# Combine weights by way of DRAM, fewer and larger loads, bias copies over three engines, layer norms applied on VectorE

## The reference

```
x = x + Xattn0(LN(x), ctx, mask)     16 heads of 8, relative bias, key mask
x = x + FFN(LN(x))                   low-rank: gelu(x U1 V1 + b1) U2 V2 + b2
x = x + Xattn1(LN(x), ctx)           16 heads of 8, no bias and no mask
x = x + MoE(LN(x))                   16 experts, hidden 64, top 8, and one shared expert
```

## Time and profile before

| | |
|---|---|
| median of three runs | 346.16 us (345.96 to 347.55) |
| the profiled execution's own time | 346.3 us |
| its span, first to last instruction | 343.8 us |
| PE busy | 182.1 us, 53% |
| DVE busy | 112.8 us, 33% |
| ACT busy | 106.7 us, 31% |
| POOL busy | 95.0 us, 28% |
| mean granted TensorE clock | 0.77 |

### The profile page before, as it was taken

One profiled execution on the slowest core, in us unless ns is written; L12 is line 12 of the kernel. 1 busy time (PEld: TensorE's weight loads), 2 busy tenths in 40 slices (PEclk: granted clock), 3 DMA queues, 4 the chain that ended last, 5 costly groups with the idle time before them and its releaser, 6 DMA issues.

```text
span 343.8 us, 4955 instructions
## 1 busy us (share of the span) xinstructions
PE 182.1 (53%) x1875; PEld 124.8 (36%) x1875; DVE 112.8 (33%) x273; ACT 106.7 (31%) x189; POOL 95.0 (28%) x179
## 2 busy tenths in 40 slices
PE   2059189849995989700089600099699200460006
PEld 1045034436652556600078500077478100450006
DVE  5224755318558457600004300037655200010000
ACT  1016556726551758600036300034543100010000
POOL 5508531014652143000295000342153000500014
PEclk9999589969995699965559965569899755585557
DMA  5796632223022112877501877511003877277760
GB/s 153 238 183 133 127 79 56 50 61 86 20 51 57 26 45 55 29 42 35 19 0 8 33 36 33 60 38 47 11 2 11 33 35 34 11 27 36 39 36 15
DMA packets 33078, 17.96 MB, mean 52 GB/s; under 512 B 12032, under 2 KB 32352, under 8 KB 33056
## 3 DMA queue, kind: packets, MB, share of 16 engines
q1 hardware_dynamic: 33056, 17.66, 46.6%
HBM read 5.04 MB, written 0.55 MB: 16 GB/s over the span
## 4 chain that ended last, share of the span: by engine, by line
PE 30%; SPq 24%; issue 22%; DMA 11%; POOL 5%; DVE 5%; ACT 2%; POOLq 0%
SPq L270 14%; PE two_s L1151 5%; DMA cbS<-combT 5%; SPq L248 5%; PE two_s L1143 4%; PE one_m L1285 4%; SPq L206 4%; PE two_s L1258 3%; PE one_m L1197 2%; DMA stack_Q<-nmT 2%; POOL hid_h L469 2%; PE one_m L1229 2%; PE one_m L1093 2%; POOL xn L424 2%; PE one_m L1119 2%
## 5 line engine op out<-in xcount | busy, mean ns | idle before, releaser
L469 POOL TENSOR_TENSOR hid_h<-hid_h,cbS 128x512 f32<-128x512 f32 x16 | 20.0, 1268 | 133.3 <-DMA cbS<-combT 133.3
L882 DVE TENSOR_REDUCE mx<-two_s 128x8 f32<-128x1024 f32 x32 | 38.1, 1220 | 50.3 <-PE two_s L1151 49.9
L1285 PE MATMUL one_m<-wd,hid_h 128*128 128x128 f32 x128 | 21.5, 332 | 57.0 <-POOL hid_h L469 57.0
L1285 PEld LDWEIGHTS one_m<-wd,hid_h 128*128 128x128 f32 x128 | 20.0, 242 | 58.5 <-POOL hid_h L469 57.3
L602 ACT ACTIVATE pt_p<-two_s 128x1024 f32<-128x1024 f32 x32 | 32.0, 1024 | 24.7 <-PE two_s L1151 24.5
L1093 PE MATMUL one_m<-ident,xn 128*128 128x128 f32 x32 | 7.4, 318 | 59.2 <-POOL xn L424 58.7
L550 ACT ACTIVATE xnT<-one_m 128x256 f32<-128x256 f32 x16 | 6.1, 383 | 70.7 <-PE one_m L1093 70.7
L1093 PEld LDWEIGHTS one_m<-ident,xn 128*128 128x128 f32 x32 | 3.8, 154 | 62.2 <-POOL xn L424 60.2
L424 POOL TENSOR_SCALAR xn<-xr,mv,rstd 128x128 f32<-128x128 f32 x32 | 25.9, 817 | 1.7
L939 DVE TENSOR_TENSOR hid_h<-hid_h,two_s 128x512 f32<-128x512 f32 x16 | 10.9, 683 | 39.2 <-ACT hid_h L640 33.9
L1197 PE MATMUL one_m<-pt_p,va 128*32 128x128 f32 x512 | 21.5, 296 | 0.2 <-ACT pt_p L602 0.2
(11 more groups left out here) (116 smaller groups left out, 325.2 us busy)
## 6 DMA issues: line engine op xcount, KB each, us to landing
cbS<-combT SPq DMA_DIRECT2D x64, 64.0 KB, 7.9
stack_K<-ksp SPq DMA_DIRECT2D x48, 64.0 KB, 2.1
stack_Q<-qsp SPq DMA_DIRECT2D x48, 64.0 KB, 2.1
cbS<-rel_bias_scratch SPq DMA_DIRECT2D x3, 224.0 KB, 4.1
wg<-in_wg SPq DMA_DIRECT2D x1, 544.0 KB, 4.0
wu<-in_wu SPq DMA_DIRECT2D x1, 544.0 KB, 4.8
xr<-in_x SPq DMA_DIRECT2D x4, 128.0 KB, 3.4
cx<-in_ctx SPq DMA_DIRECT2D x4, 128.0 KB, 2.8
```

The source lines that it names most:

```text
L469: pool.tensor_tensor(h[:].rearrange("p (c t) -> p c t", c=2), h[:].rearrange("p (c t) -> p c t", c=2), cbS[:, p % 2, 2 * u:2 * u + 2], ALU ...
L882: free(dve.tensor_reduce(mx[:, l, p % 2, b, c].rearrange("p a j -> p (a j)"), src[:].rearrange("p a (j k) -> p (a j) k", j=4), AX.X, ALU.m ...
L1285: ins = pe.matmul(dst[:, b * D:(b + 1) * D], h[:, at_col:at_col + SEQ], wd[:, 2 * u + k], start=False, stop=(n == UNITS), skip_group_check ...
```

## The change

Seven things change.

1. `combT` of a pair is stored to DRAM by one DMA (`store_weights`, 16 KB), and after that has landed two DMAs of 512 KB, each reading every second expert's row 64 times over, fill `cbS` (`spread_weights`).
2. `normalize` is parted: POOL keeps the power (`power`), DVE applies the norm, for all four norms. The forms for POOL and ACT that the text of the kernel also has (`normalize` there, `shift_of`) are called by nothing.
3. The loads are merged: identity, constants and the Q and K biases are one DMA (`first`), which ACT issues together with `wqk`; wv, wo, bv and b1 are one (`second`); the low-rank factors and the gate (`small`), wg and wu (`wgu`), wd and swd (`wdown`), pairs 1 to 3 of x and of ctx are one each. SP issues 10 loads. Context and x of pair 0 come early, `small` last.
4. The mask comes repeated over heads from DRAM, in uint8, and two DMAs that POOL issues write it as bf16 into `bias_s` and `bias_t`; the copy on DVE and the eight DMAs on SP are gone.
5. Of the eight window copies DVE makes four (two of each kind), ACT two and POOL two (one of each kind); PE waits for all three engines before the first use of each kind.
6. Four of the eight stacks are cleared on POOL instead of DVE.
7. The lists of all five engines and of the PSUM and SBUF slots are written in a new order. In POOL's, the powers of the norms of pairs 2 and 3 stand ahead of the `weigh` calls, but for `power(2, 3)`; in SP's, the stacking of Q for pair 3 stands ahead of the second spread; in PE's, the `down` calls of pair 1 stand beside the gates of pair 2.

The diff, cut to its core (the slot table and most of the reordered lists are left out):

```diff
+    comb_d = nc.dram_tensor("combine_scratch", (2, EXPERTS, TOK), F32, kind="Internal").ap()
...
+            def store_weights(p):
+                freed(sp, f"ct{p}")
+                sp.dma_start(comb_d[p % 2], combT[:, p % 2]).then_inc(sem("comb_stored"), 16)
+
             def spread_weights(p):
-                freed(sp, f"ct{p}")
+                sp.wait_ge(sem("comb_stored"), 16 * (p + 1))
                 if p >= 2:
                     sp.wait_ge(sem("weighted"), UNITS * (p - 1))
-                for e in range(EXPERTS):
-                    r = 64 * (e % 2)
-                    src = combT[e:e + 1, p % 2].unsqueeze(1).broadcast_to([1, 64, TOK])
-                    sp.dma_start(cbS[r:r + 64, p % 2, e // 2], src).then_inc(sem(f"spread{p % 2}_in"), 16)
+                for k in range(2):
+                    src = bass.AP(tensor=comb_d.tensor, offset=(p % 2) * EXPERTS * TOK + k * TOK,
+                                  ap=[[0, 64], [2 * TOK, ECH], [1, TOK]])
+                    sp.dma_start(cbS[64 * k:64 * k + 64, p % 2], src).then_inc(sem(f"spread{p % 2}_in"), 16)
...
-            load(table, table_d, "rel")
-            load(onehot, onehot_d, "rel")
-            load(wqk[:], wqk_d, "wqk")
-            load(bqk[:], bqk_d, "wqk")
+            load(rel_in, rel_in_d, "rel")
             load(rowb[:], rows_d.partition_broadcast(128), "rows")
-            load_x(0)
-            load(wv[:], wv_d, "wv")
-            load(wo[:], wo_d, "wo")
-            load(bv[:], bv_d, "wo")
-            load_x(3)
-            load_x(2)
-            load_x(1)
-            load(mask8[96:128, 0], masks_d.rearrange("(g r) k -> r g k", g=4), "mask")
-            load(mask8[96:128, 1], maskt_d.rearrange("(g r) k -> r g k", g=4), "mask")
-            load_ctx(1)
-            load_ctx(3)
-            load(u1t, u1t_d, "ffw")
-            load(v1, v1_d, "ffw")
-            load(u2t, u2t_d, "ffw")
-            load(v2, v2_d, "ffw")
-            load(b1[:], b1_d, "ffw")
-            load_ctx(2)
-            load(gate, gate_d, "gate")
-            load(wg[:], wg_d, "moe")
-            load(wu[:], wu_d, "moe")
-            load(wd[:], wd_d, "moe")
-            load(swd[HID:128], swd_d, "moe")
-            load(ident[:], ident_d, "ident")
-            load(consts[:].bitcast(U16), consts_d, "consts")
-            load_ctx(0)
+            load_x(1, 4)
             fixed_rows(0, 0)
+            load_ctx(0, 1)
+            load_x(0, 1)
+            load(second[:], second_d, "second")
+            fixed_rows(0, 1)
+            load(wgu[:], wgu_d, "wgu")
+            store_windows()
             fixed_rows(1, 0)
-            spread_masks()
-            store_windows()
-            stack("K", 0, 1, 0)
+            load_ctx(1, 4)
+            load(wdown[:], wdown_d, "wdown")
+            load(small, small_d, "small")
             stack("K", 0, 0, 0)
             load_windows()
...
+            store_weights(0)
             spread_weights(0)
-            spread_weights(1)
             stack("Q", 0, 1, 2)
             stack("Q", 1, 1, 2)
             stack("Q", 2, 1, 2)
+            store_weights(1)
             stack("Q", 0, 1, 3)
+            stack("Q", 2, 1, 3)
+            max_rows(1, 2, 0)
             stack("Q", 1, 1, 3)
-            stack("Q", 2, 1, 3)
+            spread_weights(1)
             store(0)
-            max_rows(1, 2, 0)
-            store(1)
             max_rows(1, 2, 1)
             max_rows(1, 3, 0)
             max_rows(1, 3, 1)
+            store_weights(2)
             spread_weights(2)
+            store(1)
+            store_weights(3)
             spread_weights(3)
             store(2)
             store(3)
...
+            def load_masks():
+                for t in range(2):
+                    pool.dma_start(bias["ST"[t]][96:128], masks_d[t].rearrange("r (g h k) -> r g h k", g=4, h=HEADS))\
+                        .then_inc(sem("masks_in"), 16)
...
-            def normalize(n, p):
+            def power(n, p):
                 if n == 0 and p == 0:
                     pool.wait_ge(sem("half"), 1)
                 pool.wait_ge(sem(f"variance{n}"), p + 1)
                 pool.tensor_tensor(rstd[:, p], ve[:, p], half[:], ALU.pow).then_inc(sem(f"rstd{n}"), 1)
...
-            constants()
+            negative_half()
+            clear_stack("K01")
+            clear_stack("Q01")
             clear_values(0, 0)
             clear_values(0, 1)
             scale_queries()
-            normalize(0, 0)
+            clear_max()
+            power(0, 0)
+            load_masks()
+            power(0, 1)
+            power(0, 2)
+            gate_power()
             residual(0, 0)
             residual(0, 1)
             residual(0, 2)
             residual(0, 3)
-            normalize(0, 1)
-            normalize(0, 2)
-            normalize(0, 3)
-            gate_power()
-            window_t(1)
-            window_t(3)
-            split_max(0, 0, 0)
+            window("T", 3)
+            power(0, 3)
+            window("S", 3)
+            clear_stack("K11")
+            clear_stack("Q11")
             clear_values(1, 0)
             clear_values(1, 1)
...
-            normalize(3, 0)
+            power(3, 0)
             router_norm(0)
             residual(1, 2)
-            normalize(1, 2)
+            power(1, 2)
+            residual(1, 3)
+            power(1, 3)
+            residual(2, 2)
+            power(2, 2)
+            power(3, 1)
             weigh(0, 0)
-            normalize(3, 1)
+            weigh(0, 1)
             router_norm(1)
-            residual(1, 3)
-            weigh(0, 1)
-            normalize(1, 3)
+            residual(2, 3)
             weigh(0, 2)
-            residual(2, 2)
-            normalize(2, 2)
+            power(2, 3)
             weigh(0, 3)
-            residual(2, 3)
-            weigh(1, 0)
-            normalize(2, 3)
-            weigh(1, 1)
-            weigh(1, 2)
             split_max(1, 2, 0)
-            weigh(1, 3)
             split_max(1, 2, 1)
             split_max(1, 3, 0)
+            weigh(1, 0)
+            weigh(1, 1)
             split_max(1, 3, 1)
-            normalize(3, 2)
+            weigh(1, 2)
+            power(3, 2)
+            weigh(1, 3)
             router_norm(2)
-            normalize(3, 3)
+            power(3, 3)
             router_norm(3)
             weigh(2, 0)
...
+            act.dma_start(first[:], first_d).then_inc(sem("first_in"), 16)
+            act.dma_start(wqk[:], wqk_d).then_inc(sem("wqk_in"), 16)
...
+            def normalize(n, p):
+                dve.wait_ge(sem(f"rstd{n}"), p + 1)
+                for b in range(2):
+                    ins = dve.tensor_scalar(xn[:, p, b], xr[:, p, b], mv[:, p, b, 0:1], rstd[:, p, b:b + 1],
+                                            ALU.subtract, ALU.mult)
+                ins.then_inc(sem(f"norm{n}"), 1)
...
+            clear_stack("K00")
             clear_stack("Q00")
-            clear_stack("K00")
+            clear_stack("K10")
             clear_stack("Q10")
-            clear_stack("K10")
             variance(0, 0)
-            mask_bf16()
-            value_bias()
-            clear_stack("Q01")
-            second_ffn()
             variance(0, 1)
             variance(0, 2)
+            variance(0, 3)
             gate_clamp()
-            variance(0, 3)
-            clear_stack("K01")
-            clear_stack("Q11")
-            clear_stack("K11")
-            window_s(0)
-            window_s(1)
-            window_s(2)
-            window_s(3)
+            value_bias()
+            normalize(0, 0)
+            normalize(0, 1)
+            normalize(0, 2)
             gate_scale()
+            second_ffn()
+            window("S", 0)
+            window("S", 1)
+            normalize(0, 3)
+            window("T", 0)
+            window("T", 1)
             row_max(0, 0, 0, 0)
...
+            def windows_ready(t):
+                pe.wait_ge(sem(f"bias_{t}_dve"), 2)
+                pe.wait_ge(sem(f"bias_{t}_act"), 1)
+                pe.wait_ge(sem(f"bias_{t}_pool"), 1)
...
+    on_heads = lambda m: _np.ascontiguousarray(
+        _np.broadcast_to(m.reshape(4, 32, 1, SEQ).transpose(1, 0, 2, 3), (32, 4, HEADS, SEQ))).reshape(32, -1).view(_np.uint8)
...
-        "masks": _np.ascontiguousarray(mask).view(_np.uint8),
-        "maskt": _np.ascontiguousarray(mask.T).view(_np.uint8),
+        "masks": _np.stack([on_heads(mask), on_heads(mask.T)]),
+        "first": _np.concatenate([_np.eye(128, dtype=_np.float32), bits(consts), bqk], 1),
         "wqk": _np.stack([_np.stack([by_dim(a["L0_xattn_Wq"]), by_dim(a["L0_xattn_Wk"])], 1),
```

792 lines of the change are left out of this document (409 added, 383 removed), and 37 rows, old and new, of the table SLOTS.

## The result

The changed kernel takes 207.4 to 208.0 us where the kernel before took 346.2 (ratio 0.5994, 95% interval 0.5964 to 0.6024). The median of all four is 209.9 us. The forecast of 226 us had the direction and most of the mechanism; its range, from 213 us, lay above the result. The profiled execution took 207.38 us, with a span of 205.6.

A forecast was written before the change was run, and what follows sets the result against it. It took PE's waits behind SP's slow copies of the combine weights as the bound, with PE otherwise fullest. 343.8 - 53.5 - 53.8 - 10 - 3 = 223.5 us of span, so 226 us measured; range 213 to 246.

The forecast's parts named there:

- the spread: Combine weights copied into cbS: by DRAM 10.5 us (7 to 13) instead of about 34 for the first.
- The order of POOL and SP: Powers ahead of `weigh` make the spread's speed hardly matter for the first two pairs; both idle stretches go, -53.5 us.
- the middle: Stretch of 117.8 us with 55.7 us of PE work: 64.3 us at 13.3% idle, -53.5 us (-48 to -62).
- Rival B: New lists on every engine make PE wait more, 20% of its work idle: 243 us, chance 0.14.
- The end: After pair 2's weights are there: pair 3's land sooner, ending at 290.0 instead of 343.8, -53.8 us (-49 to -57).
- The start: Loads and window copies up to the first scores, then at about 31 to 32 us: -10 us (-14 to 0).
- the mark at which the text calls itself wrong: At the start: the prediction counts as wrong if scores start after 36 us.
- The norms: 32 applications move from POOL to DVE at 0.29 us each: -3 us (+3 to -8).
- A: Spread copies reading one DRAM region go at 50 GB/s, not the load's rate: 256 us, chance 0.07.
- C: At the start, masks issued by POOL come late and the 10 us are lost: 236 us, chance 0.11.
- D: Reads of one DRAM region in the spread bound everything, slower than before: 418 us at 15 GB/s, chance 0.01.
- E: Spreads land soon but `weigh` or the norms are still held; 25 us come back: 251 us, chance 0.05.

The follow-up runs named there:

- b_filler2: The kernel before with 250 unused transposes of the identity on PE in each of its first two idle stretches: 344.85 us, ratio 0.9946.
- b_dram: The kernel before with only the spread of the combine weights changed, to go by DRAM, every list of work as it was: 247.69 us, ratio 0.7131.

## Why the forecast was right in kind and 18 us too high

- **What bounds the kernel, and the spread.** Right. Store and copies took about 8 us (forecast 10.5, bounds 7 to 13) and the copies landed 5.9 us after issue, inside the 9. That the source partition and not the bytes was the limit is shown: landing 7.7 us and issue 1.9 us out of one partition, 2.6 and 0.6 us from DRAM, both for 64 KB (medians). The Trainium skill (SBUF — State Buffer, section "Door 1: The DMA port swizzle") puts a transfer to 64 partitions at 196 GB/s; the two copies side by side, with little else, moved 242 GB/s between 126 and 128 us, so for these 2 us the two halves together went faster than that.
- **The order of POOL and SP.** "For the first two pairs the speed of the spread hardly matters" failed: with the old copies in the new order POOL still stands 106.9 us for the weights and PE 90 us behind it. The reordering moved one reader of POOL's list (the norms) ahead of `weigh` and left another (the maxima) behind it. What the reordering is worth beside the fast spread was not run by itself.
- **The failed step** is the middle: "Applied to the 55.7 us of PE, it makes 64.3 us". The idle share was right: 7.9 us idle in 55.5 measured, 8.6 forecast. PE's busy time in the stretch was mis-sized, 63.8 us taken over where 47.6 were done. Some 7 us of it was longer matmuls, most of them behind the waits; the windows of the kernel before showed the clock there (0.58, 0.50), and the forecast read this time as PE's own work. `b_filler2` shows 4.6 us of it to be the clock; for the rest that is argued from the same rows. The other part is work that no longer stood in this stretch: the `down` of pair 1 (21 more `down` matmuls in the last stretch, 2.8 us at 0.135 us each, where the forecast said 5 and did not take them out of the middle), 16 gate and up matmuls there as well (3.8 us), and 48 matmuls more ahead of 122.9 us. Rival B, which had PE idle more, looked at the other factor.
- **The end.** Right: 27.2 us for a forecast of 27.9. The last weights were there at 196.7 us, 18.3 us after the stretch began, where 18.1 was forecast; in that sum a faster spread (8 us) stood against a later store of pair 3's weights (188.0 us, 9.5 after the stretch began, not 7.6). PE was busy for 24.4 of the 27.2 us.
- **The start.** -5.8 us to the first scores, where -10 was forecast, inside the bounds but at 36.1 us just past the mark at which the text calls itself wrong. The windows landed at 25.8, not 21 us, and `small` took 11.7 us from issue at 8.5 us. Yet the weights of pair 0 came at 122.9 us as forecast (123.2): from the first scores to there it took 86.8 us instead of 94.3, with PE idle for 8.1 us of it instead of 13.6, where the forecast had 3 us for the norms. The sum is right by luck, as its two terms were off by 4 us each, in opposite directions.
- **The norms.** 3 to 4 us, as forecast. DVE's busy time rose by 14 us and not by 5, as it took 19.7 us for them where 9.3 were counted: the applications cost 0.34 us in the median, and the one beside POOL's copy and memsets 6.05.
- **POOL** lost 17.1 us of busy time, not 25; the norms took 25.9 with them, and four memsets of stacks of 1.80 us each came, 7.2 us that the sum for POOL left out though the text named them.
- Rivals A, C, D and E did not come: the copies went at 242 GB/s in their best window (about 160 from first issue to landing), the masks were never waited for, and `weigh` waited for nothing but the spread itself.

## What to carry to other kernels

When a long wait on TensorE goes altogether, take away its length and also the half-speed work behind it: read the granted clock of the 5 to 7 us after each idle stretch, and count busy time at the high level. Where the wait is only shortened, take nothing away: with waits of 3 to 6 us left, `b_dram` had all of the kernel's 182 us of busy time. Less busy time is not the same amount of time won, either (4.6 us against 1.9 in `b_filler2`).

When a start is brought forward, follow the gain engine by engine to the first result that everything waits for. Here 5.1 us at the first scores were 0.95 us at the first maxima, because DVE's list had a blocked copy and a blocked norm ahead of them. The low clock moved with the start too, and was the more visible thing; before it gets the blame, compare executions that agree in everything else.

Two edits on one chain can be worth their whole price each, if each alone leaves a different reader waiting: check every reader that stands behind the slow call in an in-order list, not only the one named by the profile.
